# Transposed inputs of a sandwich layer by transposing DMAs in place of TensorE, with attention weights and x tiles fetched at other places

## The reference

```python
x = x + LN(attn(LN(x)))      # Q, K, V = x@Wq+bq, x@Wk+bk, x@Wv+bv
x = x + LN(ffn(LN(x)))       # (silu(x@Wg.T) * (x@Wu.T)) @ Wd.T, 3072 hidden, int weights / 127

# attn: rows in segments of 512, four interleaved residues r, 16 heads of 64;
# head h uses only the rows with residue h % 4
scores = (Qs * Ks).sum(-1) / 8         # one number per row and head, no row against row
probs  = softmax(scores over the 128 rows of one residue in a segment)
out    = zeros; out[those rows, those heads] = probs * Vs
return out @ Wo + bo
```

## Time and profile before

| | |
|---|---|
| median of 3 runs | 2445.08 us (2444.38 to 2447.3) |
| the profiled execution | 2442.37 us, span on its slowest core 2440.1 us |
| spans of the 8 cores | 2424.8 to 2440.1 us |
| mean granted TensorE clock | 0.984 to 0.987 |
| busy share: TensorE matmuls, weight loads | 94%, 44% |
| busy share: VectorE, ScalarE, GpSimd | 44%, 26%, 9% |
| moved by DMA | 298.47 MB, mean 122 GB/s |

### The profile page before, as it was taken

How to read it: one execution, slowest core, us unless ns; L and a number is a source line. 1 busy time by engine, 2 the same in 40 slices (tenths; PEclk the granted TensorE clock), 3 DMA queues, 4 the chain that set the end, 5 groups by cost and what they waited for, 6 DMA issues and landing times.

```text
span 2440.1 us, 33099 instructions; the slowest of 8 cores (2424.8 to 2440.1 us)
## 1 busy us (share of the span) xinstructions
PE 2289.6 (94%) x11074; PEld 1066.9 (44%) x11296; DVE 1068.9 (44%) x1825; ACT 625.9 (26%) x832; POOL 215.0 (9%) x564
## 2 busy tenths in 40 slices
PE   3576999999999999999999999999999999999998
PEld 1232444444444444444444444444444444444443
DVE  3533344353544535354453535445354443535322
ACT  1210323223232322323223132322313232232211
POOL 1111101011010100101010010101001010010100
PEclk9799999999999999999999999999999999999999
DMA  9299152452515234262422515145251424324140
GB/s 208 58 205 212 73 170 70 155 139 81 179 61 163 88 117 143 79 183 77 163 97 95 173 61 173 69 156 130 88 180 61 164 78 147 113 82 143 70 155 35
DMA packets 83686, 298.47 MB, mean 122 GB/s; under 512 B 9664, under 2 KB 9664, under 8 KB 83520
## 3 DMA queue, kind: packets, MB, share of 16 engines
q1 hardware_dynamic: 73728, 268.47, 32.1%
q0 software_dynamic: 9216, 27.27, 7.2%
q10 hardware_dynamic: 576, 0.60, 0.1%
HBM read 277.43 MB, written 46.14 MB: 133 GB/s over the span
## 4 chain that ended last, share of the span: by engine, by line
PE 86%; DMA 6%; DVE 2%; issue 2%; POOL 1%; ACT 1%; DVEq 0%; POOLq 0%; SPq 0%; ACTq 0%
PE pf L407 25%; PE pf L403 25%; PE pf L421 24%; PE pa L342 7%; DMA gu<-wgu 3%; PE pa L381 2%; DMA gu<-scr_gu 2%; PE pt L329 1%; DMA scr_gu<-gu 1%; PE pt L336 1%; DMA x<-x 1%; DVE bn L481 1%; POOL stats L245 1%; ACT xh L703 1%; DVE bn L482 1%
## 5 line engine op out<-in xcount | busy, mean ns | idle before, releaser
L403 PE MATMUL pf<-xT,gu 128*128 128x512 bf16 x2993 | 724.5, 382 | 45.7 <-DMA gu<-wgu 32.0
L407 PE MATMUL pf<-xT,gu 128*128 128x512 bf16 x3023 | 726.0, 380 | 2.8 <-issue 0.2
L421 PE MATMUL pf<-wd_sb,h 128*128 128x512 bf16 x2994 | 675.7, 379 | 4.1
L569 DVE TENSOR_TENSOR h<-silu,pf 128x512 bf16<-128x512 bf16 x384 | 264.0, 687 | 861.8 <-PE pf L407 764.9
L731 ACT ACTIVATE silu<-pf 128x512 bf16<-128x512 f32 x384 | 229.0, 596 | 1024.3 <-PE pf L403 1024.1
L403 PEld LDWEIGHTS pf<-xT,gu 128*128 128x128 bf16 x3072 | 299.9, 98 | 409.5 <-issue 59.1
L407 PEld LDWEIGHTS pf<-xT,gu 128*128 128x128 bf16 x3072 | 301.8, 98 | 366.6 <-issue 7.4
L421 PEld LDWEIGHTS pf<-wd_sb,h 128*128 128x128 bf16 x3072 | 296.3, 98 | 338.4
L243 POOL TENSOR_SCALAR stats<-stats 128x1 f32<-128x1 f32 (+1 forms) x112 | 36.2, 323 | 2048.3 <-DVE stats L484 2048.2
L739 ACT ACTIVATE y<-pf 128x512 f32<-128x512 f32 x128 | 76.1, 594 | 407.2 <-PE pf L421 407.2
L342 PE MATMUL pa<-xT,wqkv_sb 128*128 128x512 bf16 x752 | 174.1, 382 | 1.9 <-DVE xT L496 1.1
(11 more groups left out here) (44 smaller groups left out, 889.4 us busy)
## 6 DMA issues: line engine op xcount, KB each, us to landing
gu<-scr_gu SPq DMA_DIRECT2D x360, 512.0 KB, 3.3
x<-x SPq DMA_DIRECT2D x64, 512.0 KB, 9.1
out<-x SPq DMA_DIRECT2D x64, 512.0 KB, 2.7
gu<-wgu POOLq DMA_DIRECT2D x24, 512.0 KB, 15.5
scr_gu<-gu SPq DMA_DIRECT2D x24, 512.0 KB, 9.4
wqkv_sb<-wqkv POOLq DMA_DIRECT2D x12, 512.0 KB, 12.6
wd_sb<-wd POOLq DMA_DIRECT2D x24, 256.0 KB, 18.9
wo_sb<-wo POOLq DMA_DIRECT2D x4, 512.0 KB, 21.0
```

The source lines that it names most:

```text
L403: ins = eng.matmul(g[:], gu[:, o:o + 128], half(xT3, kc), start=(kc == 0), stop=(kc == KC - 1))
L407: ins = eng.matmul(u[:], gu[:, o:o + 128], half(xT3, kc), start=(kc == 0), stop=(kc == KC - 1))
L421: ins = eng.matmul(pf[m % 4][:], h[:, 512 * kc + 128 * j:512 * kc + 128 * j + 128], wd[:, D * kc + 512 * hf:D * kc + 512 * hf + 512], star ...
L569: eng.tensor_mul(half(h, k), half(silu, k % 2), pf[2 * (k % 2) + 1][:]).then_inc(v_h, 1)
```

## The change

The identity matrix, the PSUM tiles `pt`, `t1` and `t3` on TensorE and the copies `x1` and `x3` on VectorE are gone. ScalarE issues a transposing DMA from `xh` straight to xT1 or xT3 behind each apply (`x1_turn`, `x3_turn`), once that apply is complete. `xh` has four slots; a slot is written again when the transposing DMA that reads it has landed (`d_t`). The first gate product and the first projection of a unit wait for `d_t`. `qk` and `a_bf` are gone too: the product q * k is written over `q`, and the attention output over `v`. ScalarE's order in the down phase is new: `y_evict` comes first, x3 applies follow evictions 0 and 1, x1 applies evictions 4 to 7. `load_attn` waits for the last up product and stands behind `l3(a)`. The four x loads stand one by one behind gu loads k = 10, 13, 16 and 19. The core of the diff:

```diff
-        xh = E(nc.sbuf_tensor("xh", [128, 2 * D], BF16))
+        xh = E(nc.sbuf_tensor("xh", [128, 4 * D], BF16))
...
-        qk = E(nc.sbuf_tensor("qk", [128, 2 * 512], BF16))
...
-        a_bf = E(nc.sbuf_tensor("a_bf", [128, 2 * 512], BF16))
...
-        with contextlib.ExitStack() as pctx:
-            pa = [pctx.enter_context(nc.psum_tensor(f"pa{i}", [128, 512], F32)) for i in range(4)]
-        with contextlib.ExitStack() as pctx:
-            pt = [pctx.enter_context(nc.psum_tensor(f"pt{i}", [128, D], BF16)) for i in range(4)]
+        pa = [E(nc.psum_tensor(f"pa{i}", [128, 512], F32)) for i in range(4)]
...
+        d_t = [sem(f"dt{j}") for j in range(4)]
...
         def xh_slot(j):
-            return xh[:, D * (j % 2):D * (j % 2) + D]
+            return xh[:, D * j:D * j + D]
...
                             load_gu(p + 1, k)
                             if k == 8:
                                 store(p, 3)
-                            if k == 12 and p + 3 < units:
-                                eng.wait_ge(d_o[p % 3], 64 * (p // 3 + 1))
-                                load_x(p + 3)
+                            if k in (10, 13, 16, 19) and p + 3 < units:
+                                if k == 10:
+                                    eng.wait_ge(d_o[p % 3], 64 * (p // 3 + 1))
+                                load_x(p + 3, (k - 10) // 3)
...
+                    if a < units:
+                        l3(a)
                     if a % 4 == 3 and a + 1 < units:
                         eng.wait_ge(t_w, 8 * a + 8)
+                        eng.wait_ge(t_gu, HCN * (p + 1))
                         load_attn((a + 1) // 4)
-                    if a < units:
-                        l3(a)
                     l4(p, 0)
...
-                def t1(a, j):
-                    eng.wait_ge(a_x1, 4 * a + j + 1)
-                    if a:
-                        eng.wait_ge(v_x3, 4 * (a - 1) + j + 1)
-                    for c in range(KC):
-                        ins = eng.transpose(pt[j][:, 128 * c:128 * c + 128], xh_slot(j)[:, 128 * c:128 * c + 128], ident[:])
-                    ins.then_inc(t_x1, 1)
-
-                def t3(a, j):
-                    eng.wait_ge(a_x3, 4 * a + j + 1)
-                    eng.wait_ge(v_w, 8 * a + 5 + j)
-                    for c in range(KC):
-                        ins = eng.transpose(pt[j][:, 128 * c:128 * c + 128], xh_slot(j)[:, 128 * c:128 * c + 128], ident[:])
-                    ins.then_inc(t_x3, 1)
...
                 def proj_q(a, ch):
                     if ch == 0:
-                        eng.wait_ge(v_x1, 4 * a + 4)
+                        for j in range(4):
+                            eng.wait_ge(d_t[j], 32 * a + 16)
...
                     if k == 0:
-                        eng.wait_ge(v_x3, 4 * p + 4)
+                        for j in range(4):
+                            eng.wait_ge(d_t[j], 32 * p + 32)
...
                         down(p, m)
-                        if more and m < 4:
-                            t3(a, m)
-                        if a + 1 < units and m >= 4:
-                            t1(a + 1, m - 4)
...
-                def x1(a, j):
-                    eng.wait_ge(t_x1, 4 * a + j + 1)
-                    if a:
-                        eng.wait_ge(t_v, 2 * a)
-                    eng.tensor_copy(xT_cols(xT1, j), pt[j][:].rearrange("p (c s) -> p c s", s=128)).then_inc(v_x1, 1)
...
                 def x1_apply(a, j):
                     eng.wait_ge(g_l1, a + 1)
-                    if j < 2:
-                        if a:
-                            eng.wait_ge(t_x3, 4 * (a - 1) + j + 3)
-                    else:
-                        eng.wait_ge(t_x1, 4 * a + j - 1)
+                    if a:
+                        eng.wait_ge(d_t[j], 32 * a)
                     eng.activation(
                         xh_slot(j), xrow(a, j), AF.Identity, bias=st(NM1 + j), scale=st(R1 + j)).then_inc(a_x1, 1)
 
+                def x1_turn(a, j):
+                    eng.wait_ge(a_x1, 4 * a + j + 1)
+                    if a:
+                        eng.wait_ge(t_v, 2 * a)
+                    eng.dma_start_transpose(out=xT_cols(xT1, j), in_=xh_slot(j)).then_inc(d_t[j], 16)
+
                 def x3_apply(a, j):
                     eng.wait_ge(g_l3, a + 1)
-                    if j < 2:
-                        eng.wait_ge(t_x1, 4 * a + j + 3)
-                    else:
-                        eng.wait_ge(t_x3, 4 * a + j - 1)
+                    eng.wait_ge(d_t[j], 32 * a + 16)
                     eng.activation(
                         xh_slot(j), xrow(a, j), AF.Identity, bias=st(NM3 + j), scale=st(R3 + j)).then_inc(a_x3, 1)
 
+                def x3_turn(a, j):
+                    eng.wait_ge(a_x3, 4 * a + j + 1)
+                    if a:
+                        eng.wait_ge(t_gu, HCN * a)
+                    eng.dma_start_transpose(out=xT_cols(xT3, j), in_=xh_slot(j)).then_inc(d_t[j], 16)
+
                 def q_evict(a, ch):
...
                 for j in range(4):
                     x1_apply(0, j)
-                eng.wait_ge(d_c, 64)
+                    x1_turn(0, j)
+                eng.wait_ge(d_c, 48)
...
-                    if more:
-                        x3_apply(a, 0)
-                        x3_apply(a, 1)
-                    y_evict(p, 0)
-                    if more:
-                        x3_apply(a, 2)
-                    y_evict(p, 1)
-                    if more:
-                        x3_apply(a, 3)
-                    y_evict(p, 2)
-                    ln4_apply(p, 0)
-                    y_evict(p, 3)
-                    if nxt:
-                        x1_apply(a + 1, 0)
-                        x1_apply(a + 1, 1)
-                    y_evict(p, 4)
-                    ln4_apply(p, 1)
-                    if nxt:
-                        x1_apply(a + 1, 2)
-                    y_evict(p, 5)
-                    if nxt:
-                        x1_apply(a + 1, 3)
-                    y_evict(p, 6)
-                    ln4_apply(p, 2)
-                    y_evict(p, 7)
+                    for m in range(8):
+                        y_evict(p, m)
+                        if more and m < 2:
+                            for j in (2 * m, 2 * m + 1):
+                                x3_apply(a, j)
+                                x3_turn(a, j)
+                        if nxt and m >= 4:
+                            x1_apply(a + 1, m - 4)
+                            x1_turn(a + 1, m - 4)
+                        if m in (2, 4, 6):
+                            ln4_apply(p, m // 2 - 1)
```

More of the change, by code:

```diff
@@ L172, in _, with load_x @@
             def _(eng):
-                def load_x(u):
-                    for j in range(4):
-                        b, s = rows(u, j)
-                        eng.dma_start(out=xrow(u, j), in_=x_d[b, s, :]).then_inc(d_x[u % 3][j], 16)
+                def load_x(u, j):
+                    b, s = rows(u, j)
+                    eng.dma_start(out=xrow(u, j), in_=x_d[b, s, :]).then_inc(d_x[u % 3][j], 16)
                 def store(p, j):
@@ L368, in scores @@
                         eng.wait_ge(a_v, 2 * a + 1)
-                    eng.matmul(pa[2 + ch][:], blk[:], half(qk, ch), start=True, stop=True).then_inc(t_s, 1)
+                    eng.matmul(pa[2 + ch][:], blk[:], half(q, ch), start=True, stop=True).then_inc(t_s, 1)
                 def out_proj(a, j):
@@ L438, in _ @@
                     out_proj(0, j)
-                for j in range(4):
-                    t3(0, j)
-                if units > 1:
-                    for j in range(4):
-                        t1(1, j)
                 for p in range(units):
@@ L583, in _ @@
                     ln1(0, j)
-                for j in range(4):
-                    x1(0, j)
-                eng.wait_ge(d_c, 64)
+                eng.wait_ge(d_c, 48)
                 qk_mul(0, 0)
@@ L602, in _ @@
                         ln1(1, j)
-                for j in range(4):
-                    x3(0, j)
-                if units > 1:
-                    for j in range(4):
-                        x1(1, j)
                 for p in range(units):
```

75 lines of the change are left out of this document (17 added, 58 removed).

## The result

| | before | after |
|---|---|---|
| time | 2445.1 us | 2405.3 us |
| ratio to before | | 0.9835, interval 0.9806 to 0.9864 |
| profiled execution, span | 2442.37, 2440.1 us | 2407.82, 2406.2 us |
| mean granted TensorE clock | 0.984 to 0.987 | 0.982 to 0.984 |
| start of the first down product | 239.79 us | 289.83 us |

The change is faster by 1.65%, 40 us. The prediction said 65 us (2380), with 2360 to 2475 as its range: the sign was right and the range held, but the time is 25 us above the forecast. (Times compared are of undisturbed executions only.)

The account below looks back on a forecast made before the run. TensorE, 86% of the chain of work, was taken to bound the kernel. The terms summed as 2445.1 - 51.6 - 18.7 - 11.1 + 16 = 2379.7, say 2380 us, with 2360 to 2475 as the range.

Parts of the forecast that it names:

- Removed from TensorE: Transposes between down products go, 116 batches for 51.6 us, and 15 stops for late xh, 18.7 us.
- Attention weights: Loads moved behind the last up product end stops in three units' gate and up products: 11.1 us won, nothing new waits.
- x loads, GpSimd's order, VectorE's copies at nothing: Spread x loads, GpSimd's l3 before the weight loads and l4 behind, VectorE's 128 copies removed: each costed at 0 us.
- h: Time one turn's issue holds ScalarE in steady units: 0.45 to 1.5 us; rival of longer holds, over 3.4 us, chance 0.10.
- The stream: Time one turn occupies the transposing DMA stream: 1 to 4 us; slow-stream rival, gain gone from 6.0 us, chance 0.14.
- Landing: Time until the last x1 turn's data land: 3 to 7 us, no wait; late-landing rival, 9.1 or 12.6 us, chance 0.16.
- ScalarE's margin: Down products of steady units: TensorE waits once an issue holds ScalarE 2.8 us, each further us costing 8 us a unit.
- The head: Unit 0's x1 turns meet full DMA engines, delaying the first projection 0.5 to about 30 us; 16 taken.
- -2 to +4 us, taken as 0: Gate product 0 in the head starts at 95.5 to 100 us, before at 97; counted as no change.
- The first projection near 52 us: Sign to look for in the head of the profile after: TensorE's first projection starts near 52 us, before at 36.08.
- B: Theory of the experiments, about the head: the first turns of a program are slow by themselves; no chance given.
- C: Theory of the experiments: the head is late because x and weight loads come in another order or pace; no chance given.

Follow-up runs that it names:

- the run with two turns: The changed kernel with a second, unused transposing DMA of the same tile behind each turn of the steady units: 2512.5 us.
- the quiet head with wd first: The quiet head with all 24 wd loads at the start instead of 16 of them between the gu loads: 2358.5 us.
- the quiet head: Changed kernel with unit 0's gate, up and down weight loads waiting for its four x1 turns, and unit 1's x1 turns moved behind unit 0's exponentials: 2369.4 us.

## Why the prediction was right, and where it was wrong

**Removed from TensorE: right.** 51.6 us for 116 batches and 18.7 for 15 stops. With the 11.1 of the loads the sum was 81.4 us; the body wins 83.6 us on the profiled core and 79 on the median core. The unit of 138.6 us is measured as 138.56, and no down product waits.

**Attention weights: right in the sum.** Predicted 11.1; alone in the kernel before 10.7 to 11, inside the changed one 8 to 10. That "nothing new waits" holds for TensorE; that the loads would meet the x3 turns and hold ScalarE some 6 us in three units was not foreseen, and only ScalarE's spare time hid it.

**x loads, GpSimd's order, VectorE's copies at nothing: right** for the first, by its own run. The other two were not changed alone; the timeline shows no wait on the path that would be theirs.

**The turns in steady units: right.** h was taken as 0.45 to 1.5 and is 1.25 (one turn in each of three units at some 6). The stream was taken as 1 to 4 us a turn; packets say 1.5. Landing was taken as 3 to 7 and is 3.0. The rule of the Trainium skill (VectorE: DVE Perf Modes, "The three transpose paths"), 1309 ns a block and by estimate 10.5 us a turn, does not hold here: eight blocks land in 3.0 us, issue included. Another page of it (Advanced Engine Details and Errata, "X-Bar Transpose (TRN2)") calls transposing DMAs as fast as plain ones, and with 1.5 us a turn against the 0.7 us of the same bytes in 4 KB packets the trace lies nearer to that.

**ScalarE's margin: wrong, without effect.** The step was (47.4 - 4.9 - 20.2) / 8 = 2.8 us. The first eviction ends its wait 5.5 us after the down products' start, not 4.9, and in the run with two turns the last holds are longer than the others, where gu loads run again (1.62 and 3.95 us). The two runs with extra turns put the point near 1.9. The price beyond it, 8 us a unit for each us, came out: 11.3 us for 1.40, which is 8.1. One constant h was the flaw of the step, and it is the flaw of the next.

**The head: wrong, the term that failed.** The prediction put it so: "At worst they go at the pace of bo [...] until the crowd ends near 62 us: about 30 us later. I take 16." It was 50.0 on the profiled core and 41 on the median core. At the first projection 32.4 us were lost (35.4 by the medians), beyond the bound: the worst case was given as data that land late, and all four turns were thought to be in flight together. In fact the issue itself is held (23.17 and 7.31 us), so that the third and fourth turn, and their applies, begin only when the crowd is ending. Of the term "-2 to +4 us, taken as 0" 2.3 came. And a part had no term at all: between gate product 0 and the first down product, 15.3 us on this core, 5 to 6 by the medians. ScalarE's list there (four x3 and four x1 applies, each with a turn, then the first silu) was read off the diff for steady units only, where evictions lie between; in the head the eight stand back to back, 23 us of ScalarE from 119.48 to 142.57, and the x1 turns have landed only 15 us behind the last issue, beside the gu loads that have begun again. With the x1 turns moved ahead both stops were gone. "The first projection near 52 us" was the sign to look for, and at 68.50 it failed. Sum: 16 taken, 50.0 measured, 34 us too few, of which the body gave 2 and the tail's rest 1 back. These 31 us are what the two profiled executions miss (34.6 us apart, 65.4 forecast). By the times it is 25, and the medians over the cores come near it: 41 where 16 was taken, and 79 won where 81.4 was forecast, 27 together.

**Settled and open.** That long issues come from the traffic is shown by three runs: short issues as soon as the loads wait, long ones at 63 to 101 us when a long crowd is put there, in the quiet head with wd first most clearly; the holds of some 6 us beside the attention weights in the changed kernel agree. B and C are refuted. Full engines alone do not settle how long an issue takes: 1.99 us at a share of 1.07, and 2.01 us at 1.17 as a crowd was ending. How the holding comes about is argued only. A turn gives each of 16 engines 66 packets (1056 / 16). If an engine takes one packet of the turn, then one 4 KB packet (175 ns) of each other queue that has work, the turn needs 66 x 0.175 = 11.6 us beside one full queue and 23 us beside two. With GpSimd's loads alone in flight 10.05 and 11.06 were measured. Beside the holds of 12.70 and 13.51 us SP's stores to scr_gu are still landing at first, and beside that of 23.17 they come from 35.19 us on. SP's queue, in the changed kernel and in the quiet head:

```profile
35.19 14.67 SPq L185 DMA_DIRECT2D scr_gu<-gu  x4
```
```profile
47.31 13.45 SPq L186 DMA_DIRECT2D scr_gu<-gu  x4
```

These stores land some 9.6 us after their issue, so to about 59 and 70 us. The Trainium skill (DMA: Bandwidth & Descriptors, "Queues, rings and completion order") says that an engine takes its queues in turn, packet by packet; the numbers agree with it, if each packet of the profile is one of the page's packets, which can hold several descriptors; no run shows that. But why the issue holds ScalarE, and not only the landing, and why the first turn of a row passes in 1.4 to 2.2 us, no run was made to tell. Some 2 us by the medians (144.5 against 142.4; 5 on the profiled core) between gate product 0 and the first down product of the quiet head are unexplained too.

## What to carry to other kernels

A DMA is not free for the engine that issues it: cost its issue at the level of traffic at that moment, not as one number, and above all where many small packets meet full DMA engines. A change that is priced on the steady loop must be walked through the head once more by each engine's own list, since work that lies between other work in the loop may stand back to back there. And two parts of one change may meet: loads that were moved off one engine's way landed here among the new turns. The two ways may also be mixed: transposes by TensorE in the head, where it idles and DMA is full, and by DMA in the loop, where it is the other way round, beat either one alone by 46 us and more.

## What the runs showed of the hardware

- A transposing DMA of 128x1024 bf16 from SBUF to SBUF is 1056 packets of 23 ns; it holds ScalarE 1.25 us and lands after 3.0 us by the median of the changed kernel, 3.3 us with 24 of them in a unit.
- The same issue took 5.7 to 10.1 us beside the four attention weight loads, and 7 to 23 us in the head's crowd of weight loads (share 1.06 to 1.12). The first turn of a row took 1.3 to 2.2 us even then.
- Four turns whose issues ended at 142.57 had all landed only at 157.89, with the DMA engines at a share of 1.04 from 150 to 158 us.
- A stop of 1.25 us left TensorE's pace alone before; behind the stop of 3.96 us in the run with two turns 16 matmuls took 6.29 us between starts in place of 3.45. The granted clock in that stretch is the lower level, 0.50 (1.2 GHz):

```profile
478.00:484.00 6.00, 5.71 (x14) 2.11 (x15) 2.23 (x5) 1.72 (x2) 1.40 (x5) 0.50 0.27 77
```

So a stop of 4.0 us cost its unit 7.0 (145.54 - 138.56).
